# A fused transformer block on one core: in its linear attention each group's front one tile earlier, the normalised queries ahead of the mask, and parts of the second group's front moved into the seam

## The reference

```python
qkv = x @ W_attn + b_attn           # x is the layer-normalised input
q = elu(q) + 1; k = elu(k) + 1      # 16 heads of 8
def step(carry, inp):
    kv = kv + kt[..., :, None] * vt[..., None, :]
    ksum = ksum + kt
    num = jnp.einsum('bhi,bhij->bhj', qt, kv)
    den = jnp.einsum('bhi,bhi->bh', qt, ksum)[..., None] + EPS
    return ((kv, ksum), num / den)
x = x + y @ W_proj + b_proj
```

## Time and profile before

| | |
|---|---|
| median of three runs | 670.46 us |
| profiled execution, its own time | 669.73 us |
| its span in the trace | 667.9 us |
| mean granted TensorE clock | 0.959 |
| busy: PE, DVE, ACT, POOL | 590.3, 481.9, 352.5, 305.4 us |
| linear attention: first scores to scores of tile 28 | 392.5 to 546.0 us |

### The profile page before, as it was taken

The page is one execution under the profiler, slowest core; times in us unless marked ns, Lnnn a source line. Parts: engine busy times, 40 slices in busy tenths (PEclk is TensorE's granted clock), DMA queues, the critical chain, the costliest instruction groups (busy, mean ns, idle before and its releaser), DMA issues.

```text
span 667.9 us, 14023 instructions
## 1 busy us (share of the span) xinstructions
PE 590.3 (88%) x5407; PEld 432.9 (65%) x5407; DVE 481.9 (72%) x1009; ACT 352.5 (53%) x658; POOL 305.4 (46%) x353
## 2 busy tenths in 40 slices
PE   4989998899999969969999768899888987799996
PEld 3878885566666659947777635555555654377775
DVE  6868886576666627799998536676766667799972
ACT  5642331344444431379987523444444535799973
POOL 6522111222233222567886653444444334477763
PEclk9989999799999999999999768998899888799999
DMA  9500000000000010000000000000000000000011
GB/s 251 113 1 2 1 2 1 1 1 2 1 1 2 1 34 1 1 0 2 1 1 1 0 1 1 2 2 1 1 2 1 1 2 1 0 18 23 27 32 31
DMA packets 15908, 9.56 MB, mean 14 GB/s; under 512 B 1446, under 2 KB 15718, under 8 KB 15844
## 3 DMA queue, kind: packets, MB, share of 16 engines
q1 hardware_dynamic: 15844, 8.68, 5.0%
HBM read 6.59 MB, written 2.10 MB: 13 GB/s over the span
## 4 chain that ended last, share of the span: by engine, by line
PE 50%; DVE 22%; ACT 9%; POOL 9%; issue 7%; DMA 1%; POOLq 0%; SPq 0%; DVEq 0%; ACTq 0%
PE ps L1225 6%; PE ps L1473 5%; PE ps L1365 4%; PE ps L1406 4%; PE ps L1241 4%; PE ps L1382 3%; PE ps L1492 3%; PE ps L1387 3%; DVE r L859 3%; DVE m L899 3%; PE ps L1232 3%; POOL G L313 3%; ACT S L525 2%; DVE arena L1078 2%; ACT qbd L551 2%
## 5 line engine op out<-in xcount | busy, mean ns | idle before, releaser
L371 POOL TENSOR_TENSOR A<-S,r 126x512 f32<-126x512 f32 x36 | 37.7, 1048 | 145.0 <-DVE r L862 132.7
L406 POOL TENSOR_SCALAR_AFFINE_SELECT arena<-arena 128x1024 f32<-128x1024 f32 x32 | 34.9, 1092 | 75.9 <-ACT arena L696 75.9
L313 POOL TENSOR_TENSOR G<-S,hoff 128x704 f32<-128x704 f32 x32 | 48.6, 1520 | 31.0 <-DVE S L995 29.0
L1382 PE MATMUL ps<-wguT,xnt 128*128 128x352 f32 x128 | 52.4, 492 | 10.9 <-ACT xnt L609 9.5
L1406 PEld LDWEIGHTS ps<-wdT,xnt 128*128 128x128 f32 (+1 forms) x384 | 51.3, 196 | 9.6 <-ACT xnt L616 3.6
L1406 PE MATMUL ps<-wdT,xnt 128*128 128x128 f32 (+1 forms) x384 | 55.0, 280 | 2.6 <-ACT xnt L616 2.6
L1078 DVE TENSOR_TENSOR arena<-ps,XN 128x1024 f32<-128x1024 f32 x32 | 39.2, 1224 | 25.0 <-PE ps L1473 25.0
L696 ACT ACTIVATE arena<-ps 128x1024 f32<-128x1024 f32 x32 | 32.7, 1023 | 39.8 <-PE ps L1473 39.8
L859 DVE TENSOR_REDUCE r<-S 126x16 f32<-126x512 f32 x36 | 24.7, 685 | 32.6 <-ACT S L525 32.6
L1387 PE MATMUL ps<-wguT,xnt 128*128 128x352 f32 x128 | 44.4, 471 | 0.0
L529 ACT ACTIVATE arena<-ps 128x456 f32<-128x456 f32 x36 | 19.9, 552 | 42.4 <-PE ps L1241 42.4
(11 more groups left out here) (201 smaller groups left out, 1513.0 us busy)
## 6 DMA issues: line engine op xcount, KB each, us to landing
X<-in_x SPq DMA_DIRECT2D x8, 256.0 KB, 5.3
out<-X SPq DMA_DIRECT2D x8, 256.0 KB, 2.3
arena<-in_wqkvT SPq DMA_DIRECT2D x4, 256.0 KB, 5.2
band<-in_band SPq DMA_DIRECT2D x1, 897.8 KB
arena<-in_wqkvT SPq DMA_DIRECT2D x1, 512.0 KB, 8.7
early<-in_wfc SPq DMA_DIRECT2D x1, 512.0 KB, 10.2
kI<-in_scaled_eye SPq DMA_DIRECT2D x1, 192.0 KB
XN<-in_wattn SPq DMA_DIRECT2D x1, 192.0 KB, 2.5
```

The lines of the kernel that those rows point to most:

```text
L313: tt(out=hgrid, in0=hmoved[k], in1=hoff[k][:, :], op=ALU.subtract).then_inc(s["fh_grid"], 1)
L371: tt(out=A1v[:, w % NW, :].rearrange("p (h m) -> p h m", m=M), in0=S1v[:, w % NW, :].rearrange("p (h m) -> p h m", m=M), in1=r1[:, 3, w % ...
L1382: mm(ps[:, GATE_BANK, 0:F], xT[t // QD % 2][:, t % QD, :], wguT[:, 0:F], start=True, stop=True).then_inc(s["f_gate"], 1)
```

## The change

No arithmetic changes, and no instruction is added or taken away. Phases 1, 2 and 3 of a front become phases 0, 1 and 2, and its step 1 moves to phase 3 of the group before. PE runs the denominators ahead of the attention of its tile, and their transposes (step 7) at the end of the same iteration. DVE's `lin_qbd` is split: `lin_qn` stands ahead of the next mask, the four masked copies where `lin_qbd` stood. In the seam, PE runs the denominators of group 0 ahead of the last `down` products, and step 1 and the query product of group 1 ahead of the first scores. The transposes of group 1 go to bank B instead of A.

```diff
@@ -424,7 +428,9 @@
                     lin_cap(0, ek, "lin_ek_done", "lin_ek_capped")
                 if r == 16:
                     lin_bias(0)
+            lin_cap(1, eq, "lin_eq_done", "lin_eq_capped")
             lin_select(0)
+            lin_cap(1, ek, "lin_ek_done", "lin_ek_capped")
             layernorm_moments(2, QN - 1)
             lin_bias(1)
             for n in range(TILES):
@@ -432,12 +438,12 @@
                 if n + 1 < TILES:
                     lin_select(n + 1)
                 if q < TILES // QD:
-                    if phase == 1:
+                    if phase == 0:
                         lin_cap(q, eq, "lin_eq_done", "lin_eq_capped")
                         lin_cap(q, ek, "lin_ek_done", "lin_ek_capped")
-                    if phase == 2:
+                    if phase == 1:
                         lin_qk(q)
-                    if phase == 3 and q + 1 < TILES // QD:
+                    if phase == 2 and q + 1 < TILES // QD:
                         lin_bias(q + 1)
                 if n % QD == 1 and n > QD:
                     layernorm_moments(3, n // QD - 1)
...
@@ -711,27 +721,31 @@
                 if r == 14:
                     lin_xbT(0)
                 if r == 15:
-                    lin_exps(0)
+                    lin_exp_q(0)
+                    lin_exp_k(0)
                     lin_norm(1)
                 if r == 16:
                     lin_pk(0)
-                if r == 17:
-                    lin_spread(0)
+            lin_xbT(1)
+            lin_exp_q(1)
             lin_raw(0)
-            lin_xbT(1)
+            lin_exp_k(1)
             for n in range(TILES):
                 q, phase = (n + 1) // QD + 1, (n + 1) % QD
                 if n + 1 < TILES:
                     lin_raw(n + 1)
                 if q < TILES // QD:
                     if phase == 0:
-                        lin_xbT(q)
-                    if phase == 1:
-                        lin_exps(q)
-                    if phase == 2:
+                        lin_exp_q(q)
+                        lin_exp_k(q)
+                    if phase == 1 and n > 0:
                         lin_pk(q)
+                    if phase == 3 and q + 1 < TILES // QD:
+                        lin_xbT(q + 1)
                 lin_yT(n)
-                if q + 1 < TILES // QD and phase == 3:
+                if n == 0:
+                    lin_pk(q)
+                if q + 1 < TILES // QD and phase == 1:
                     lin_norm(q + 1)
                 if q < TILES // QD and phase == 2:
                     lin_spread(q)
...
@@ -1063,10 +1077,12 @@
                 need(v, "lin_rden_spread", q)
                 recip(out=rden, in_=den).then_inc(s["lin_rden_done"], 1)
 
-            def lin_qbd(q):
+            def lin_qn(q):
                 v.wait_ge(s["lin_rdenT_done"], q + 1)
                 need(v, "lin_num_done", (q - 1) * QD)
                 tt(out=qn[q % 2], in0=ps[:, FRONT_A, :], in1=phq[q % 2], op=ALU.mult).then_inc(s["lin_qn_done"], 1)
+
+            def lin_qbd(q):
                 v.wait_ge(s["lin_qn_done"], q + 1)
                 for h in range(HR):
                     last = ts(out=qbd[q % 2][:, h, :], in0=qn[q % 2], scalar1=rowhead[:, h:h + 1], scalar2=None, op0=ALU.mult)
@@ -1103,6 +1119,9 @@
             v.wait_ge(s["att_x_done"], TILES)
             tile_stats(1, TILES - 1)
             for r in range(PN + 3):
+                if r == PN + 2:
+                    lin_qn(0)
+                    lin_qbd(0)
                 step0(r)
                 if r == 14:
                     v.wait_ge(s["b_loaded"], 16 * 8)
@@ -1116,28 +1135,31 @@
                     lin_v(0)
                 if r == 17:
                     lin_den(0)
-                if r == 18:
-                    lin_qbd(0)
             lin_mask(0)
             for n in range(TILES):
                 q, phase = (n + 1) // QD + 1, (n + 1) % QD
                 if n > 0:
                     lin_out(n - 1)
+                if q < TILES // QD and phase == 3:
+                    lin_qn(q)
                 if n + 1 < TILES:
                     lin_mask(n + 1)
                 if n > 0:
                     lin_stats(n - 1)
                 if q < TILES // QD and phase == 3:
                     lin_qbd(q)
+                if q < TILES // QD and (phase == 0 or n == 0):
+                    lin_phi(q)
                 if q < TILES // QD and phase == 1:
-                    lin_phi(q)
+                    lin_scan(q)
+                    if n > 0:
+                        lin_v(q)
                 if q < TILES // QD and phase == 2:
-                    lin_scan(q)
-                    lin_v(q)
+                    lin_den(q)
                 if (n + 1) % NT:
                     lin_state(n)
-                if q < TILES // QD and phase == 2:
-                    lin_den(q)
+                if n == 0:
+                    lin_v(q)
                 if n in LIN_FILL:
                     step1(LIN_FILL[n])
             lin_out(TILES - 1)
...
@@ -1428,15 +1450,18 @@
 
             def lin_transposes(q):
                 pe.wait_ge(s["lin_xb_done"], q + 1)
-                need(pe, "lin_qn_done", q)
+                need(pe, "lin_den_copied" if q == 1 else "lin_qn_done", q)
                 for k in range(QD):
-                    last = tp(ps[:, FRONT_A, k * P:(k + 1) * P], xb[:, k, :], eye[:, :])
+                    last = tp(ps[:, turn_bank(q), k * P:(k + 1) * P], xb[:, k, :], eye[:, :])
                 last.then_inc(s["lin_xT_done"], 1)
 
-            def lin_qk_mms(q):
+            def lin_q_mm(q):
                 pe.wait_ge(s["lin_xbT_copied"], q + 1)
                 need(pe, "lin_den_copied", q)
                 mm(ps[:, FRONT_B, :], wattn[:, 0:P], xbT, start=True, stop=True).then_inc(s["lin_q_done"], 1)
+
+            def lin_k_mm(q):
+                need(pe, "lin_qn_done", q)
                 mm(ps[:, FRONT_A, :], wattn[:, P:2 * P], xbT, start=True, stop=True).then_inc(s["lin_k_done"], 1)
 
             def lin_v_mms(q):
@@ -1512,21 +1537,24 @@
             for r in range(PN + 3):
                 if r < 2:
                     pe.wait_ge(s["att_x_done"], TILES - 1 + r)
+                if r == 17:
+                    lin_den_mms(0)
                 step0(r)
                 if r == 13:
                     pe.wait_ge(s["fx_moved"], ffn_quads(0, QN))
                     lin_transposes(0)
                 if r == 14:
                     pe.wait_ge(s["f_silu"], ffn_tiles(0, TILES))
-                    lin_qk_mms(0)
+                    lin_q_mm(0)
+                    lin_k_mm(0)
                 if r == 15:
                     lin_v_mms(0)
-                if r == 17:
-                    lin_den_mms(0)
             lin_rdenT(0)
+            lin_transposes(1)
+            lin_q_mm(1)
             pe.wait_ge(s["fh_moved"], ffn_pairs(0, PN))
             lin_scores(0)
-            lin_transposes(1)
+            lin_k_mm(1)
             pe.wait_ge(s["f_x_done"], PN)
             for n in range(TILES):
                 q, phase = (n + 1) // QD + 1, (n + 1) % QD
@@ -1534,19 +1562,22 @@
                 if n + 1 < TILES:
                     lin_scores(n + 1)
                 if front and phase == 0:
-                    lin_transposes(q)
-                if front and phase == 1:
-                    lin_qk_mms(q)
+                    lin_q_mm(q)
+                    lin_k_mm(q)
+                if front and phase == 1 and n > 0:
+                    lin_v_mms(q)
                 if front and phase == 2:
-                    lin_v_mms(q)
-                if front and phase == 3:
-                    lin_rdenT(q)
+                    lin_den_mms(q)
+                if front and phase == 3 and q + 1 < TILES // QD:
+                    lin_transposes(q + 1)
                 lin_attend(n)
                 if (n + 1) % NT:
                     lin_state_mm(n)
+                if n == 0:
+                    lin_v_mms(q)
+                lin_proj(n)
                 if front and phase == 2:
-                    lin_den_mms(q)
-                lin_proj(n)
+                    lin_rdenT(q)
                 if n in LIN_FILL:
                     step1(LIN_FILL[n])
             for r in range(PN + 3):
```

More of the change, by code:

```diff
@@ L229, in up_banks, with turn_bank @@
             return ps[:, 1 + 2 * (r % 2):3 + 2 * (r % 2), start:start + width]
+        def turn_bank(q):
+            return FRONT_B if q == 1 else FRONT_A
         def lin_states(n):
@@ L655, in step @@
                         offset_h(r)
+                    if p == 0 and r == PN + 1:
+                        lin_spread(0)
                     if 0 <= r - 2 < PN:
@@ L671, in lin_xbT, with lin_exp_q @@
                 need(a, "lin_v_done", q)
-                act(xbT, ps[:, FRONT_A, :], ACT.Copy).then_inc(s["lin_xbT_copied"], 1)
-            def lin_exps(q):
+                act(xbT, ps[:, turn_bank(q), :], ACT.Copy).then_inc(s["lin_xbT_copied"], 1)
+            def lin_exp_q(q):
```

(1 more changed line is left out.)

## The result

The changed kernel takes **654.87 us** (median of 4, 652.37 to 655.61) against 670.18 us before (median of 4). The ratio is 0.9756, interval 0.9729 to 0.9783. A second series of runs of the same two kernels gave 654.1 us (6 runs, 650.67 to 655.33) and 0.9737 (0.9705 to 0.9768). The profiled execution took 655.61 us, 14.1 less than that of before; its span is 653.7 us. The forecast was 652.5.

A forecast was written before the change was run, and what follows sets the result against it. PE was taken to bound the stage, at small distance. Fronts 14.4 less 1.3 for clock, seam and first group 7.9 less 1.3, sum 19.7; less 1.8 for handoffs, 17.9 us saved: 652.5 us, range 647 to 660.

The forecast's parts named there:

- Phases 0 and 1: Steady front's first two iterations: queries, keys and exponentials 5.10 us; values, scan and product 4.72 us.
- Phase 2: Steady front's third iteration, denominators and transposed reciprocals: PE floor 4.68 us plus waits of 0.11 and 0.20, sum 4.99.
- that rival: Fronts: a new wait at the end of phase 2 replaces the old, only 2.3 to 5 us stay, 665 to 668; chance 0.08.
- Two of the signs that the forecast named: Profile after, steady fronts: scores of a new group wait 0.5 to 0.8 us for `qbd`; a front takes 19.2 to 19.8.
- phase 3: Steady front's last iteration, `qn`, mask and `qbd`: scores come 0.71 us earlier than 5.17, so 4.46 us.
- The allowances for the clock: One clock fall put back in the six fronts, 1.3 us, and one in the seam and first group, 1.3 us.
- handoffs: Six steady fronts: 0.3 us allowed for each, 1.8 us, for handoffs that a schedule leaves out.
- the forecast's 9.4: First group: scores of tile 0 at 390.2 us, denominators of group 1 at 399.6, with POOL setting the pace.
- the rival in which they go on without the stalls: Fronts and first group: stalls go but the clock keeps falling, one fall per front; 10.1 us less, 660; chance 0.18.
- a slower one: Whole kernel: the change makes it slower; chance 0.06.
- The seam: Before the first scores: denominators of group 0 go into PE's idle gap before `down`, transposes begin 2.3 us earlier.
- 0.68 + 0.18 + half of 0.08: Chance that the kernel is faster, from forecast, falling-clock case and half of the third, given as 0.91.

The follow-up runs named there:

- the best version: Changed kernel with one masked copy moved ahead of the mask and POOL's phase 3 select waiting for the masked copies: 645.13 us, 0.9611.
- the last edit: POOL's moments and bias put behind the product of group 1, in the changed kernel with first copy ahead of mask and select behind copies: 647.84 us, 0.9653.

## Why the prediction was right, point by point

**The steady fronts.** Phases 0 and 1 were forecast 5.10 and 4.72 and took 5.11 and 4.71. Phase 2, 4.99, took 5.10, and not for its waits: PE is idle 0.09 us in it, less than the 0.31 allowed. It is the transposed reciprocals that take 0.59 us to the next scores (445.78 to 446.37), where the forecast had 0.49, and the attention's first products (L1510) that take 0.39 (443.39 to 443.78) where they took 0.32 in the iteration the sum was built on (438.76 to 439.08 in the kernel before). The denominators' wait fell below 0.3 us as said, but for group 1 (1.67); both edits that undo a step of this part lose most of it or a good part (9.3 us of the fronts' 10.9 with `lin_qn` late, 6.3 with the denominators late). No new wait took the place of the old one, which excludes that rival. Two of the signs that the forecast named failed, both by the term below: the wait for `qbd` is 1.10 and not 0.5 to 0.8, and a front takes 19.85 us, just above 19.2 to 19.8.

**The term that was mis-sized** is phase 3, "4.46 us", with its reason: "The scores come 0.71 us earlier than the 5.17". They came 0.23 earlier; it measured 4.94. The forecast took the duration of the four copies (1.67) from a place where POOL was idle and moved them to one where its select runs. 6 x 0.48 = 2.9 us, which the select behind the copies gave back entirely in the stage (fronts 119.11 to 115.99). The same collision stands in the first group: there the scan met POOL's residual product, and the select then met the scan and took 2.01 us instead of 1.09, as the timeline of the kernel after shows:

```profile
398.23 1.27 POOL L395 TENSOR_TENSOR X<-X,XN 128x512 f32<-128x512 f32 x1
...
398.84 1.74 DVE L1059 TENSOR_TENSOR_SCAN arena<-lnc,arena 128x512 f32<-128x512 f32 x1
399.46 2.01 POOL L410 TENSOR_SCALAR_AFFINE_SELECT arena<-arena 128x1024 f32<-128x1024 f32 x1
...
402.76 1.07 PE L1481 MATMUL ps<-headones,arena 128*128 128x16 f32 x8 [1.67 <-POOL arena L405]
...
411.60 1.14 PE L1498 MATMUL ps<-qbd,arena 32*128 32x512 f32 x8 [1.10 <-DVE qbd L1088]
```

The denominators of group 1 came 10.20 us after the first scores, not the forecast's 9.4, and tile 4 another 8.84 later, not 8.4. The sum of the stage is right, -18.0 against -17.9, by luck: two errors cancel. The allowances for the clock (1.3 and 1.3) and for handoffs (1.8), 4.4 in all, were not needed as such. Against them stand 2.9 us for the copies under the select and 0.6 for phase 2 in the fronts, and 1.2 in the first group, less the 0.4 by which the seam came out better. How much of the 1.2 is collision was not isolated; the select's 0.92 and the copies' 0.48 lie in it.

**The clock.** One fall was left in the fronts by the forecast and none is there: the granted clock is 1.00 in all six, in the changed kernel and in those that shorten phase 3. With an idle of 2.41 us in five fronts (`lin_qn` late) there are two falls: four of the six fronts are at 0.95 to 0.97, and the clock over the fronts is 0.97; with 1.25 us in each (denominators late) two as well, the last two fronts at 0.92, and 0.97. In the fronts of these kernels falls came only where such a stall (1.02 to 2.41 us, beside the wait for `qbd`) was, and the rival in which they go on without the stalls is excluded for this kernel; the ratio of 0.9756 excludes a slower one. They don't hang on a stall or its length alone: the kernel before, with 1.58 us in each, has four of its six fronts at 0.92 and two at 1.00, and with the denominators late four fronts with 1.25 us are at 1.00. What else they hang on was not shown. Of the stage's 18 us, 9.2 are PE's busy time; the granted clock is 1.00 in the fronts where it was 0.95, and 1.00 between tiles 0 and 4 where it was 0.77, and the scores of tile 0 take 1.14 us at 1.00 where they took 2.09 at 0.50. The forecast had them in the sum (its durations for the fronts were from rows at 0.99 and 1.00), but didn't say that they are half of it.

No run shows by itself the 1.3 us at which the forecast prices a fall. It was my estimate from one iteration of the kernel before: the one from 409.92 to 415.94, at a granted clock of 0.72, lasted 6.02 us with 0.60 of waiting, so 5.42 of work, against 5.17 - 1.07 = 4.10 at 1.00. In its place the traces show whole fronts: in the kernel before PE is busy 19.83 to 19.98 us in one at 0.92 and 18.43 in the first, at 1.00, that is 1.4 to 1.6 more, and the front is 21.59 to 22.27 us long against 21.26, 0.3 to 1.0 more.

**The seam.** Forecast 2.3 us between entry and first scores, measured 2.7 to 2.8. With it taken out the kernel is 5.0 us longer in its stretch of the trace; the totals (0.9806 and 0.9737, overlapping intervals) point the same way without showing it. Alone in the kernel before it shows nothing in the total.

**What was not foreseen** is 2.7 us before the entry and 1.0 behind tile 28, in unchanged code. The forecast's "the gain is carried to the end" holds within a few us only: over all traces the entry lies between 376.0 and 380.0 and the tail is between 120.9 and 124.2 us. That is where the forecast and the median part (652.5, 654.87). A small slip in the chances changes nothing: 0.68 + 0.18 + half of 0.08 is 0.90, not 0.91.

**Open.** Whether the entry is moved by the program or by chance: the same program before gave 376.85 and 377.86, the seam alone gave 379.6 and 380.0, but POOL's product moved in the kernel before, which leaves the seam as it was, 379.6 as well, the best version 376.0, and the changed kernel with its seam undone 376.3. A part of it arises at the very start: the first products of `xl` with `wqkv` begin at 24.96 us in the kernel before and at 26.16 in the changed one, in code that is the same. Open is also whether the last edit makes a long tail more frequent.

## What to carry to other kernels

When an operation is moved, look up what runs on the neighbouring engine at its new place, and take its duration from a row with the same neighbour: a gap that a moved instruction leaves is filled by the next one, here by copies that slid under a select. Read a stretch by busy and idle time apart: with POOL's product ahead of its select, which shortened an idle of 1.58 us to 1.11, the fronts lost 1.3 us of idle time and 2.9 of busy time, and the seam alone, which saved 4.3 us up to tile 4, lost 1.3 to 2.3 of them again in fronts at 0.94 and 0.91. Where a bank is shared between two steps of a pipeline, move its reader together with its next writer; here the writer waited 2.41 us where the reader had stayed behind.

## What the runs showed of the hardware

**What two engines in each other's way cost.** In the rows of these kernels a DVE copy takes 0.47 us alone and 0.97 or 0.92 when POOL's select began before it; the scan 1.28 without a select beside it and 1.75 with one; the select 1.09 alone and 2.01 when the scan began before it. In these rows the wait stands as duration of the one that came second, not as idle time. What then remains of the second after the first one's end is its own time less 0.20 us: the copy ends at 430.21, the select before it at 429.93, so 0.28 behind it (alone 0.47); the select of the first group ends 0.89 behind the scan (alone 1.09). For the scan of the earlier trace rows the select beside it is the second of these rows of the kernel before, the first being the one beside `qn` in the earlier trace rows:

```profile
434.36 1.09 POOL L406 TENSOR_SCALAR_AFFINE_SELECT arena<-arena 128x1024 f32<-128x1024 f32 x1 [1.98 <-ACT arena L696]
...
448.40 1.09 POOL L406 TENSOR_SCALAR_AFFINE_SELECT arena<-arena 128x1024 f32<-128x1024 f32 x1 [2.84 <-ACT arena L696]
```

The select ends at 449.49, the scan at 450.56, 1.07 behind it (alone 1.28). So an overlap in these kernels is priced from rows: end of the first, plus the second's own time, less 0.20. I had taken the distance of the two ends, 1.08 us, for the scan's own time; without the select beside it the scan took 1.28. The other row shows an operation that wasn't held up: `qn`, which reads `ps` and `arena`, began at 434.76 in the middle of the select and took 0.67 us, against 0.69 in the changed kernel, where no select ran beside it. What makes the one wait and not the other no run here isolates.

**Unchanged code moves by microseconds.** Between executions of one kernel lie up to 8 us (664.81 to 673.12 with the seam alone), and the traces put them ahead of the entry (376.0 to 380.0 us) and behind tile 28 (120.9 to 124.2, at clocks of 0.98 to 0.94), while the fronts repeat to 0.06 us in the kernel before (130.01 and 130.07) and in the changed one (119.11 and 119.06); with the seam alone they took 131.34 and 132.27, at 0.94 and 0.91. A comparison of stretches between fixed instructions told the effect of an edit far closer than the totals.
